# Two matrix stages of a graph network in 512-wide products instead of pairs of 256-wide ones

## The reference

```
h = relu(Dn * H @ (Be * H.T @ (x @ W1.T)) + b1);  h = layer_norm(h) * gamma + beta
y = Dn * H @ (Be * H.T @ (h @ W2.T)) + b2 + x
x1 = layernorm(x + y)
agg = (adj @ x1) / max(rowsum(adj), 1e-6)
out = layernorm(x1 + relu(concat(x1, agg) @ W.T))
```

## Time and profile before

| | us |
|---|---|
| median of the runs | 1051.77 |
| the profiled execution | 1051.42 |
| its span | 1049.6 |
| TensorE busy | 1039.2 (99%) |
| VectorE busy | 776.7 (74%) |
| ScalarE busy | 433.3 (41%) |
| GpSimd busy | 435.6 (41%) |
| mean granted TensorE clock | 0.999 of full speed |

### The profile page before, as it was taken

The page is one execution under the profiler, slowest core; times in us unless marked ns, Lnnn a source line. Parts: engine busy times, 40 slices in busy tenths (PEclk is TensorE's granted clock), DMA queues, the critical chain, the costliest instruction groups (busy, mean ns, idle before and its releaser), DMA issues.

```text
span 1049.6 us, 19643 instructions
## 1 busy us (share of the span) xinstructions
PE 1039.2 (99%) x6241; PEld 933.2 (89%) x6241; DVE 776.7 (74%) x1848; ACT 433.3 (41%) x1029; POOL 435.6 (41%) x674
## 2 busy tenths in 40 slices
PE   8999999999999999999999999999999999999997
PEld 8889898898989989899898998989889898888986
DVE  6878786787867878677786778676786777867355
ACT  5553523445234442445325362254622536225350
POOL 0357416434254433534344353543525534265320
PEclk9999999999999999999999999999999999999999
DMA  8065431734227441274414644044440634400001
GB/s 296 3 138 117 98 90 34 152 92 103 64 59 156 96 98 31 60 160 100 90 30 87 133 100 100 20 114 106 100 100 20 142 78 100 110 11 1 2 1 40
DMA packets 72032, 90.01 MB, mean 86 GB/s; under 512 B 15544, under 2 KB 61248, under 8 KB 72000
## 3 DMA queue, kind: packets, MB, share of 16 engines
q1 hardware_dynamic: 63232, 85.49, 35.1%
q10 hardware_dynamic: 8768, 4.10, 1.7%
HBM read 81.14 MB, written 8.42 MB: 85 GB/s over the span
## 4 chain that ended last, share of the span: by engine, by line
PE 99%; DMA 0%; DVE 0%; issue 0%; ACT 0%; DVEq 0%
PE bank L1077 45%; PE bank L1107 12%; PE bank L1183 11%; PE bank L1231 11%; PE bank L1212 3%; PE bank L1219 3%; PE bank L1274 3%; PE bank L1267 3%; PE bank L1268 3%; PE bank L1211 3%; PE bank L1248 1%; PE bank L1068 1%; PE bank L1234 1%; DMA raw<-in_adj_dram 0%; PE bank L1172 0%; DVE xres L779 0%
## 5 line engine op out<-in xcount | busy, mean ns | idle before, releaser
L1077 PE MATMUL bank<-yv,adjT 128*128 128x257 f32 x1024 | 223.3, 379 | 0.0
L1077 PEld LDWEIGHTS bank<-yv,adjT 128*128 128x128 f32 x1024 | 193.6, 189 | 28.7
L566 ACT ACTIVATE small<-mv,small 128x1 f32<-128x1 f32 x192 | 56.0, 291 | 247.8 <-DVE mv L785 144.6
L1077 PE MATMUL bank<-x_hi,H 128*128 128x256 f32 x512 | 125.1, 286 | 0.0
L1231 PE MATMUL bank<-gW2T,hT 128*128 128x257 f32 x512 | 123.7, 385 | 0.0
L1107 PE MATMUL bank<-x_hi,H 128*128 128x258 f32 x512 | 123.6, 289 | 0.0
L1077 PE MATMUL bank<-x_lo,H 128*128 128x256 f32 x512 | 122.4, 280 | 0.0
L1077 PE MATMUL bank<-m_hi,HT 128*128 128x256 f32 x512 | 122.0, 281 | 0.0
L1077 PE MATMUL bank<-m_lo,HT 128*128 128x256 f32 x512 | 121.4, 279 | 0.0
L1107 PE MATMUL bank<-x_lo,H 128*128 128x256 f32 x512 | 119.2, 282 | 0.0
L561 ACT ACTIVATE m_hi<-bank,small 128x256 fp32r<-128x256 f32 x128 | 57.5, 474 | 136.2 <-DVE small L835 75.6
(11 more groups left out here) (132 smaller groups left out, 2203.1 us busy)
## 6 DMA issues: line engine op xcount, KB each, us to landing
raw<-in_adj_dram SPq DMA_DIRECT2D x112, 256.0 KB, 5.8
adjB<-in_adj_dram SPq DMA_DIRECT2D x224, 128.0 KB, 3.1
x_in<-in_x_dram SPq DMA_DIRECT2D x31, 256.0 KB, 6.1
out_dram<-xres SPq DMA_DIRECT2D x108, 64.0 KB, 1.6
raw<-in_adj_dram SPq DMA_DIRECT2D x8, 512.0 KB, 8.8
w_row<-in_adj_dram SPq DMA_DIRECT2D x8, 512.0 KB, 4.7
w_row<-rDn_row ACTq DMA_DIRECT2D x7, 512.0 KB, 9.0
out_dram<-xres SPq DMA_DIRECT2D x4, 256.0 KB, 2.1
```

Source lines behind the costliest of these rows:

```text
L566: nc.scalar.activation(std[:, i:i + 1], mv[:, which, i, 1:2], ACT.Sqrt, bias=eps_c)\
L1077: last = mm(bank(stage, i)[:, 0:n_cols], lhsT, rhs, start=(k == 0 and part == 0), stop=(k == NT - 1 and part == parts - 1))
```

## The change

S1 of the graphs after the first, and S3 but for its last tile, multiply H by x's low and high parts side by side, `x_both`, in one product of 512 columns; the bank then holds both products side by side. The two halves are joined outside: ScalarE takes `m_part` = high half * rBe, VectorE adds the low half * rBe into `m_sum` and empties the bank, ScalarE rounds `m_sum` to `m_hi`, and GpSimd subtracts to get `m_lo`. S3's tile 7 keeps its two 256-wide products and is taken at once as before. The count for Be comes, for the later graphs, from a sum that the HT operation writes beside its rows. b2 is added to xres in Q, behind each x_lo of GpSimd, and the doubling of x stands between the m_lo subtractions beside S1. S2's and S4's waits count the new m_lo (`m_split`), and SP waits for the doubled x. The WL and x1 tiles that lie in the same memory get new places.

```diff
         HT, HT_at, _ = place("HT", [P, NT, C], F32R)
-        x_hi, _, _ = place("x_hi", [P, NT, DP], F32R)
-        x_lo, x_lo_at, _ = place("x_lo", [P, NT, D], F32R)
-        m_hi, m_hi_at, _ = place("m_hi", [P, NT, D], F32R)
-        m_lo, m_lo_at, _ = place("m_lo", [P, NT, D], F32R)
+
+        x_both, _, _ = place("x_both", [P, NT, 2 * D + 2], F32R)
+        x_lo, x_hi = x_both[:, :, 0:D], x_both[:, :, D:D + DP]
+        m_both, m_at, m_end = place("m_both", [P, NT, 2 * D], F32R)
+        m_hi, m_lo = m_both[:, :, 0:D], m_both[:, :, D:2 * D]
+
+        m_f32, _, _ = place("m_f32", [P, NT, 2 * D], F32, m_at)
+        m_part, m_sum = m_f32[:, :, 0:D], m_f32[:, :, D:2 * D]
         x_in, _, _ = place("x_in", [P, NT, D], F32)
         xres, xres_at, _ = place("xres", [P, NT, D], F32)
...
                         load_graph(b + 1)
-                    sp.wait_ge(xb_ready, b * NT + NT)
+                    sp.wait_ge(xb_part, b * NT + NT)
...
-            def residual(b):
-
-                for t in range(NT):
-                    nc.gpsimd.tensor_tensor(xres[:, t, :], x_in[:, t, :], x_in[:, t, :], ALU.add).then_inc(xb_part, 1)
-                add_b2(b)
-
-            def add_b2(b):
-                for t in range(NT):
-                    pool.wait_ge(xb_part, b * NT + t + 1)
-                    nc.gpsimd.tensor_tensor(xres[:, t, :], xres[:, t, :], b2_row[:, :], ALU.add).then_inc(xb_ready, 1)
+            def double_x(t):
+                nc.gpsimd.tensor_tensor(xres[:, t, :], x_in[:, t, :], x_in[:, t, :], ALU.add).then_inc(xb_part, 1)
+
+            def take_m_lo(e, b, n):
+                pool.wait_ge(m_hi_done, b * (2 * NT) + (n + 1))
+                nc.gpsimd.tensor_tensor(m_lo[:, e, :], m_sum[:, e, :], m_hi[:, e, :].bitcast(F32), ALU.subtract).then_inc(m_split, 1)
+
+            def add_b2(t, b):
+                pool.wait_ge(xb_part, b * NT + t + 1)
+                nc.gpsimd.tensor_tensor(xres[:, t, :], xres[:, t, :], b2_row[:, :], ALU.add).then_inc(xb_ready, 1)
             def shift_of(norm, which, rstd, shift, scaled, done, i, b):
                 pool.wait_ge(rstd_done[norm], b * NT + i + 1)
...
                                             ALU.subtract).then_inc(q_split, 1)
-                if first:
-                    pool.wait_ge(bias_loaded, 16)
-                    add_b2(0)
+                    if first and i == 0:
+                        pool.wait_ge(bias_loaded, 16)
+                    add_b2(i, b)
+                for e in range(NT - 1):
+                    take_m_lo(e, b, NT + e)
                 for d in range(ND):
...
-                    pool.wait_ge(out_stored, b * OUT_B + OUT_0)
-                    residual(b + 1)
+                    for e in range(NT):
+                        take_m_lo(e, b + 1, e)
+                        if e == 1:
+                            pool.wait_ge(out_stored, b * OUT_B + OUT_0)
+                        if e > 0:
+                            double_x(e - 1)
+                    double_x(NT - 1)
             graph(0, True, True)
             with pool.Fori(1, B - 1) as b:
...
-            def take_m_hi(stage, e, b, n):
-
+
+            def take_m_hi_at_once(stage, e, b):
+                act.wait_ge(*full(stage, e, b))
+                act.wait_ge(rBe_ready, b * NT + e + 1)
+                nc.scalar.activation(m_hi[:, e, :], bank(stage, e)[:, 0:D], ACT.Identity, scale=rBe[:, e:e + 1])\
+                  .then_inc(m_hi_done, 1)
+
+
+            def take_m_part(stage, e, b):
                 act.wait_ge(*full(stage, e, b))
                 act.wait_ge(rBe_ready, b * NT + (e + 1 if stage == "S1" else NT))
-                nc.scalar.activation(m_hi[:, e, :], bank(stage, e)[:, 0:D], ACT.Identity, scale=rBe[:, e:e + 1])\
-                  .then_inc(m_hi_done, 1)
+                nc.scalar.activation(m_part[:, e, :], bank(stage, e)[:, 0:D], ACT.Identity,
+                                     scale=rBe[:, e:e + 1]).then_inc(m_part_done, 1)
+
+            def take_m_hi(stage, e, b):
+                act.wait_ge(*emptied(stage, e, b))
+                nc.scalar.activation(m_hi[:, e, :], m_sum[:, e, :], ACT.Copy).then_inc(m_hi_done, 1)
             def root(norm, which, std, i, b):
                 act.wait_ge(var_done[norm], b * NT + i + 1)
...
                 take_x_hi(NT - 1)
-                for e in range(NT):
-                    take_m_hi("S3", e, b, NT + e)
+                take_m_part("S3", 0, b)
+                for e in range(NT - 1):
+                    if e + 1 < S3_GROUP:
+                        take_m_part("S3", e + 1, b)
+                    elif e >= S3_GROUP:
+                        take_m_part("S3", e, b)
+                    take_m_hi("S3", e, b)
+                take_m_hi_at_once("S3", NT - 1, b)
...
                     for e in range(NT):
-                        take_m_hi("S1", e, b + 1, e)
+                        take_m_part("S1", e, b + 1)
+                        take_m_hi("S1", e, b + 1)
             over_graphs(act, graph)
...
-            def take_m_lo(stage, e, b, n):
-
-                dve.wait_ge(m_hi_done, b * (2 * NT) + (n + 1))
+            def take_m_lo_at_once(stage, e, b):
+                dve.wait_ge(m_hi_done, b * (2 * NT) + (e + 1 if stage == "S1" else NT + e + 1))
                 empties_bank(nc.vector.scalar_tensor_tensor(
                     out=m_lo[:, e, :], in0=bank(stage, e)[:, 0:D], scalar=rBe[:, e:e + 1],
                     in1=m_hi[:, e, :].bitcast(F32), op0=ALU.mult, op1=ALU.subtract), stage, e)
+
+            def add_m_parts(stage, e, b):
+                dve.wait_ge(m_part_done, b * (2 * NT - 1) + (e - NT + 1 if stage == "S1" else e + 1))
+                empties_bank(nc.vector.scalar_tensor_tensor(
+                    out=m_sum[:, e, :], in0=bank(stage, e)[:, D:2 * D], scalar=rBe[:, e:e + 1],
+                    in1=m_part[:, e, :], op0=ALU.mult, op1=ALU.add), stage, e)
             def build_HT_columns(c):
                 for half in range(2):
...
                 dve.wait_ge(adjT_ready, (b - 1) * NT + NT)
-                nc.vector.tensor_scalar(HT[:, k, :], adjT[:, k, :], 0.0, None, ALU.not_equal).then_inc(HT_ready, 1)
+                nc.vector.tensor_scalar(HT[:, k, :], adjT[:, k, :], 0.0, None, ALU.not_equal, ALU.add,
+                                        accum_out=be_sum[:, k:k + 1]).then_inc(HT_ready, 1)
...
-            def take_rBe(e, b):
-
-                dve.wait_ge(*full("S1", e, b))
-                nc.vector.tensor_scalar(be_safe[:, e:e + 1], bank("S1", e)[:, D:D + 1], 1.0, None, ALU.max)\
-                  .then_inc(be_done, 1)
+            def take_rBe(e, b, count):
+                nc.vector.tensor_scalar(be_safe[:, e:e + 1], count, 1.0, None, ALU.max).then_inc(be_done, 1)
                 dve.wait_ge(be_done, b * NT + e + 1)
                 nc.vector.reciprocal(rBe[:, e:e + 1], be_safe[:, e:e + 1]).then_inc(rBe_ready, 1)
...
                         next_Dn(DN_BEFORE[e], unread)
-                    take_m_lo("S3", e, b, NT + e)
+                    if e < NT - 1:
+                        add_m_parts("S3", e, b)
+                take_m_lo_at_once("S3", NT - 1, b)
                 next_Dn((NT - 1,), unread)
...
                         build_HT_rows(e, b + 1)
+                        dve.wait_ge(HT_ready, b * NT + NT + e + 1)
+                        take_rBe(e, b + 1, be_sum[:, e:e + 1])
                         if e >= 1:
-                            take_rBe(e - 1, b + 1)
-                            take_m_lo("S1", e - 1, b + 1, e - 1)
-                    take_rBe(NT - 1, b + 1)
-                    take_m_lo("S1", NT - 1, b + 1, NT - 1)
+                            add_m_parts("S1", e - 1, b + 1)
+                    add_m_parts("S1", NT - 1, b + 1)
             over_graphs(dve, graph)
...
-            def tiled(stage, b, n_cols, ready, parts, operands, group=2, behind_k=None, before_last=None):
+            def tiled(stage, b, n_cols, ready, parts, operands, group=2, behind_k=None, before_last=None,
+                      narrow=()):
                 def one(i, k):
-                    for part in range(parts):
+                    n_parts, width = (2, D) if i in narrow else (parts, n_cols)
+                    for part in range(n_parts):
                         lhsT, rhs = operands(k, i, part)
-                        last = mm(bank(stage, i)[:, 0:n_cols], lhsT, rhs, start=(k == 0 and part == 0),
-                                  stop=(k == NT - 1 and part == parts - 1))
+                        last = mm(bank(stage, i)[:, 0:width], lhsT, rhs, start=(k == 0 and part == 0),
+                                  stop=(k == NT - 1 and part == n_parts - 1))
                     if k == NT - 1:
                         fills_bank(last, stage, i)
...
+                if c == NT - 1:
+                    fills_bank(last, "S1", e)
+
+            def s1_wide_step(e, c):
```

(55 more changed lines are left out.)

17 lines of the change are left out of this document (8 added, 9 removed).

## The result

The changed kernel takes 1053.83 us (median of 17 runs, 1053.42 to 1054.08) beside 1051.77 for the kernel before (17 runs): a ratio of 1.0019, 95% interval [1.0013, 1.0026]. So it is slower, by some 2.1 us (0.2%). Its profiled span is 1051.8 us, 2.2 more than before. The number forecast, 1052.8, is 1.0 us off and its sign is right; the way there is not.

A forecast was written before the change was run, and what follows sets the result against it. TensorE, busy 99% of the span and holding 99% of the chain, was taken to bound the kernel. -2.8 + 0.7 + 3.15 = +1.05 us took 1051.77 to 1052.8 us; overall range 1048.9 to 1056.6, the forecast's own 1051.1 to 1054.6.

The forecast's parts named there:

- TensorE's gain: In S1 and S3, one 512-wide product costs less than a pair: -1.5 us and -1.3 us, together -2.8 us.
- Rival C: In S1 and S3, wide products bring nothing because x's parts lie 514 apart; stalls remain: +2.1, 1053.9 us; chance 0.05.
- Hand-over S1 to S2: HT with its row sum (1.26 us) uses up the spare time; S2 stalls 0.1 us a graph, +0.7 us.
- Rival B: Beside S1, HT is slower than a sum and VectorE's step sets S2: +5.6, 1057.4 us; chance 0.18.
- Hand-over S3 to S4: GpSimd's subtractions and VectorE's Dn sums exclude each other; m_lo(6) stalls S4's seventh step 0.45 us a graph, +3.15 us.
- The race at 471.9: Beside S3, GpSimd's m_lo(2) (471.9) against VectorE's sum 4 (471.95); either order leaves m_lo(6) 0.2 to 0.6 us late.
- A: Rival: both hand-overs, S1 to S2 and S3 to S4, fit; only -2.8 us stays, 1049.0 us; chance 0.27.
- Costed at nothing: Extra ScalarE copies, GpSimd subtractions and b2's move cost 0; ScalarE's and GpSimd's load matters only at the hand-overs.
- b2 in Q: GpSimd's b2 row fits into 0.67 us idle before the last x_lo; otherwise at most 0.7 us a graph.
- The sum: Whole kernel: -2.8 + 0.7 + 3.15 = +1.05 us, median from 1051.77 to 1052.8 us.

## Why the prediction was right in its number and wrong in its way

- **TensorE's gain**, forecast -2.8, is -4.2 (-2.5 in S1, -1.7 in S3). The mechanism holds; the size was taken from S2 (0.2334), where products go two by two to a bank. In S1 and in S3's single tiles, where all eight go to one bank and each has a new moving operand, they take 0.230 to 0.231. S1 is nothing else: 64 x 0.0024 = 0.15, the difference between the 15.13 forecast and 14.97. Rival C is out: the wide products work although x's parts lie in rows of 514.
- **Hand-over S1 to S2**, forecast +0.7, is +1.05. HT with its sum, the step and the gap at the last step came as forecast; the doubling that stands between two m_lo's was left out of the chain. Without the sum the gap is gone, as worked out. Rival B's HT of 1.36 did not come. The Trainium skill, "SBUF — State Buffer", section "Who interferes with whom", has it that a tensor_scalar that writes its accumulator stays out of the two-port modes; the trace agrees (1.20 to 1.22 everywhere with the sum, 0.68 alone and 1.00 beside a doubling without it).
- **Hand-over S3 to S4**, forecast +3.15, is 0. This is one of the two terms that failed. That the engines exclude each other came true: m_lo(2), issued 0.01 us behind a sum, took 1.80 (472.64), and m_lo(6) ran into the last sum as forecast and took 1.41 (477.80), so that it ended 0.6 behind that sum. What failed is the time at which all this stood. The race at 471.9 was won by the sum by that 0.01 us, and it ran without delay (472.63, 1.22). Later sums were held up by 0.14 and 0.20, and m_lo(6) ended 2.56 us into S4. The forecast had it at 2.80 even with the sum first, and wanted 2.60 (2.70 with the signal) for "in time": by its own need it was in time by 0.04. A chain of ten links with so little to spare could not be settled on paper; the chance given to A (0.27) was for both hand-overs, and this one alone deserved more.
- **Costed at nothing**, forecast 0, is +5.75. This is the other term that failed, and the larger one. The sentence that GpSimd's load "matters only at the hand-overs below" was wrong. The working stopped at S4's start, as if m_lo(6) were the last in its queue. Behind it stand WL_low, WL_cross and the shifts, and behind the shifts ScalarE's roots and VectorE's tiles of x1. The earlier trace rows held the hint: WL_low at 477.28, followed straight by what the first shift waits for. The experiments show it from three sides: moved, the loss is gone (1047.06); made alone in the kernel before, it is there (S4 + V 28.98); with two H tiles fewer, most is gone with the shift as late as before.
- **b2 in Q** was costed at nothing if it fits into 0.67 us of idle time. For S3's eighth step it does. But it holds up the sum by 0.4, as the working had it (0.5), and with what follows the centring by 0.46; that is 0.46 a graph.
- **The sum.** +1.05 forecast, +2.1 measured. Two errors of opposite sign, a stall of 3.15 that did not come and a loss of 5.75 that wasn't seen, and a gain taken 1.4 too small. The number was near by luck; the sign rests on the unseen term: without it the rest of the measured terms gives -3.2.

## What to carry to other kernels

When work is moved to an engine that is half idle, follow its queue past the first consumer: what stands behind the moved operations, who waits for that, and whether the engine at the end has slack to catch up. Then look for an operation in that queue with a later need, and order the queue by need. Here one such move was worth 6.8 us behind the change and nothing ahead of it, so a change that loses should be looked through for the one wait that eats its gain before it is given up.
